# Turned keys of a gated delta-rule chunk loop stored per tile in the key stage and loaded back

## The reference

```
q = silu(hs @ Wq + bq);  k = silu(hs @ Wk + bk);  v = silu(hs @ Wv + bv)
q, k = each scaled to length 1 per head
for every token t, per batch and head (S_f, S_s are 64 x 64):
    S_f = fd_t * S_f;             S_s = sd_t * S_s
    err_f = v_t - k_t @ S_f;      err_s = v_t - k_t @ S_s
    S_f += b_t * outer(k_t, err_f);  S_s += b_t * outer(k_t, err_s)
    S_fc = cap(S_f + rf * S_s);   S_sc = cap(S_s + rf * S_f)
    o_t = fg_t * (q_t @ S_fc) + sg_t * (q_t @ S_sc)
    S_f, S_s = S_fc, S_sc
```

## Time and profile before

| | |
|---|---|
| median of three runs | 3439.89 us (3428.99 to 3453.76) |
| the profiled execution | 3432.23 us, span 3430.6 us |
| PE, PEld, DVE, ACT, POOL busy | 83%, 58%, 74%, 47%, 36% of the span |
| mean granted clock | 0.928 |
| key stage | about 658 to 838 us |
| chunk loop | about 840 to 2400 us |
| DMA | 290.81 MB, mean 85 GB/s |

### The profile page before, as it was taken

One profiled execution on the slowest core, in us unless ns is written; L12 is line 12 of the kernel. 1 busy time (PEld: TensorE's weight loads), 2 busy tenths in 40 slices (PEclk: granted clock), 3 DMA queues, 4 the chain that ended last, 5 costly groups with the idle time before them and its releaser, 6 DMA issues. The chain is left out here.

```text
span 3430.6 us, 74926 instructions
## 1 busy us (share of the span) xinstructions
PE 2858.1 (83%) x28151; PEld 1973.1 (58%) x28151; DVE 2554.0 (74%) x4553; ACT 1598.3 (47%) x3575; POOL 1238.9 (36%) x1882
## 2 busy tenths in 40 slices
PE   0565999685999999999999999999484459998888
PEld 0343544364777777777777777777372443333323
DVE  8897588794787868787787868766597347777775
ACT  1222799784344444444444444434252335555554
POOL 0000233312565656666565656655464230000000
PEclk9876999896999999999999999999697779999999
DMA  1001465686123132323323232222472521011111
GB/s 31 0 0 52 166 246 234 256 259 162 34 74 68 38 83 64 78 44 74 67 71 56 53 83 63 66 45 64 148 259 75 157 60 20 20 29 20 20 26 27
DMA packets 487658, 290.81 MB, mean 85 GB/s; under 512 B 402907, under 2 KB 447515, under 8 KB 478493
## 3 DMA queue, kind: packets, MB, share of 16 engines
q1 hardware_dynamic: 478080, 256.61, 27.5%
q10 hardware_dynamic: 4608, 16.78, 1.6%
q0 software_dynamic: 4608, 12.59, 1.1%
HBM read 155.92 MB, written 129.97 MB: 83 GB/s over the span
## 5 line engine op out<-in xcount | busy, mean ns | idle before, releaser
L2388 DVE TENSOR_REDUCE mx<-banks 128x2 f32<-128x1024 f32 (+3 forms) x384 | 358.2, 955 | 146.0 <-PE banks L1839 95.2
L2080 ACT ACTIVATE probs<-banks 128x1024 f32<-128x1024 f32 (+3 forms) x384 | 309.9, 810 | 257.1 <-PE banks L1864 143.8
L1116 ACT COPY xs<-banks 64x64 f32<-64x64 f32 (+2 forms) x640 | 166.2, 260 | 397.9 <-PE banks L958 394.8
L828 POOL TENSOR_SCALAR xc<-xc,halves 128x64 f32<-128x64 f32 (+1 forms) x256 | 193.9, 757 | 359.4 <-DVE xc L1299 346.5
L958 PE MATMUL banks<-xc,ssm 64*64 64x16 f32 (+2 forms) x5120 | 249.9, 217 | 37.1 <-issue 35.0
L958 PEld LDWEIGHTS banks<-xc,ssm 64*64 64x64 f32 x5120 | 209.7, 135 | 116.4 <-issue 57.7
L1718 PE MATMUL banks<-wproj,xnT 128*128 128x512 f32 x512 | 265.4, 600 | 0.9 <-DVE sb_tok L2165 0.9
L1589 POOL TENSOR_TENSOR prj_sq<-prj 128x1024 f32<-128x1024 f32 x32 | 77.6, 2424 | 490.7 <-ACT prj L1983 490.7
L1299 DVE SCALAR_TENSOR_TENSOR xc<-xc,halves,banks 64x64 f32<-64x64 f32 (+1 forms) x512 | 160.0, 312 | 110.8 <-PE banks L969 104.7
L1106 ACT COPY ssm<-banks 16x64 f32<-16x64 f32 (+2 forms) x896 | 215.9, 241 | 50.4 <-PE banks L930 38.3
L1141 ACT COPY ah<-banks 128x768 f32<-128x768 f32 x128 | 102.2, 798 | 254.4 <-PE banks L990 254.4
(11 more groups left out here) (352 smaller groups left out, 6744.7 us busy)
## 6 DMA issues: line engine op xcount, KB each, us to landing
proj_s<-prj SPq DMA_DIRECT2D x32, 2048.0 KB, 6.7
qkv_t<-proj_s SPq DMA_DIRECT2D x32, 1536.0 KB
ka<-proj_s ACTq DMA_DIRECT2D x32, 512.0 KB, 4.5
mem_s<-o_sb SPq DMA_DIRECT2D x32, 512.0 KB, 2.6
om<-mem_s SPq DMA_DIRECT2D x32, 512.0 KB, 3.8
om<-proj_s SPq DMA_DIRECT2D x32, 512.0 KB, 4.8
nblk_s<-ssa POOLq DMA_DIRECT2D x32, 256.0 KB, 4.2
blk_s<-res SPq DMA_DIRECT2D x16, 512.0 KB, 4.3
```

The lines of the kernel that those rows point to most:

```text
L828: pool.tensor_scalar(inverse_of(k, lv + 1)[:, :, w:2 * w], inverse_of(k, lv), halves[:, lv, 1:2], None, ALU.mult).then_inc(half_set, 1)
L1116: last = act.copy(xs[right, k % 2, 0:4 * (SUB << lv)], products(k, lv, out_)[right, :])
L2080: act.activation(probs[:, s % 2, :, at:at + w], slot_of((kind, s, k))[:, :, 0:w], ACT.Exp, scale=D1 ** -0.5).then_inc(b_read, 1)
L2388: dve.tensor_reduce(mx[:, s % 2, c, :, t:t + 1].rearrange("p e a -> p (e a)"), slot_of((kind, s, k))[:, :, 0:w], AX, ALU.max).then_inc(a_r ...
```

## The change

In the key stage the turned keys, which lie in `kta` anyway, are stored by POOL to a new DRAM tensor `kt_s`, 512 KB per tile. POOL's order becomes: turned keys of tile i, blocks of tile i. ACT waits, before it overwrites a buffer of `kta`, for the store of the tile two before. SP loads the turned keys of tile i (512 KB, in pieces of 512 bytes) into `kqt`, which now holds two whole tiles (16 KB per partition in place of 4 KB; the spare tensor above shrinks so that addresses behind it stay). It does so for tiles 0 and 1 at the end of its table work in the key stage, and for each later tile directly behind the tokens. `turn` makes the two transposes of the queries alone, and `keep_turned` copies 256 columns in place of 512. The scores still read keys and queries side by side.

```diff
+        kt_s = dram("kt_s", (T, P, HD))
-        kqt = sb("kqt", [P, 2, 2, 2, P], scope=sT)
+        kqt = sb("kqt", [P, 2, 4, 2, 2, P], scope=sT)
+        kt_out = stepped
-        TILE_IN = 16 * (6 + 3 * NB)
+        TILE_IN = 16 * (7 + 3 * NB)
+            def load_turned(i):
+                sp.dma_start(kqt[:, i % 2, :, :, 0, :].rearrange("p g a t -> p (g a) t"), kt_s[i].rearrange("p (g t) -> p g t", t=P)).then_inc(tile_in[i % 2], 16)
...
                 sp.dma_start(pcb[64 * e:64 * e + 64, :], pc_s[e, :, :, :].rearrange("t h q -> (t h q)").partition_broadcast(64)).then_inc(pc_in, 16)
+            for i in range(2):
+                sp.wait_ge(kt_out[i], 16)
+                load_turned(i)
             end_phase(sp)
...
             def load_tile(i):
                 load_tokens(i)
+                load_turned(i)
                 load_right(i)
...
                 sp.wait_ge(av_mm, 4 * i - 4)
+                sp.wait_ge(y_mm, 4 * i - 4)
                 sp.wait_ge(s_new, 4 * i - 4)
...
         def chunk_pool(pool):
...
             for i in range(T):
                 n = i % 2
+                pool.wait_ge(kt_kept, 2 * i + 2)
+                pool.dma_start(kt_s[i], kta[:, n, :]).then_inc(kt_out[n], 16)
                 pool.wait_ge(ss_kept, 8 * i + 8)
...
             for n in range(2):
                 pool.wait_ge(nblk_out[n], 16 * (T // 2))
+                pool.wait_ge(kt_out[n], 16 * (T // 2))
             end_phase(pool)
+            for x in kt_out:
+                pool.sem_clear(x)
...
+            def turned(k):
+                return kqt[:, k // 4 % 2, k % 4, :, :, :]
...
             def turn(k):
...
-                for w, at in ((1, 0), (0, 1)):
-                    for p in range(2):
-                        first_col = w * HD + P * (2 * g + p)
-                        last = pe.transpose(cols(bk[1], 2 * p + at), qkv_t[:, n, first_col:first_col + P], ident[:, :])
+                for p in range(2):
+                    last = pe.transpose(cols(bk[1], p), qkv_t[:, n, P * (2 * g + p):P * (2 * g + p) + P], ident[:, :])
...
             def keep_turned_keys(i):
...
                 if i >= 2:
                     act.wait_ge(ss_mm, 2 * i - 2)
+                    act.wait_ge(kt_out[i % 2], 16 * (i // 2))
...
             def keep_turned(k):
...
-                if k >= 2:
-                    act.wait_ge(kq_mm, k - 1)
-                    act.wait_ge(y_mm, k - 1)
-                act.copy(kqt[:, y, :, :, :].rearrange("p a w t -> p (a w t)"), bk[1]).then_inc(kq_kept, 1)
+                if k >= 8:
+                    act.wait_ge(y_mm, k - 7)
+                act.copy(kqt[:, i % 2, k % 4, :, 1, :], bk[1][:, 0:2 * P].rearrange("p (a t) -> p a t", t=P)).then_inc(kq_kept, 1)
```

More of the change, by code:

```diff
@@ L153, in layer_kernel @@
         sA.close()
-        SPARE = 3280
+        SPARE = 208
         sG = ExitStack()
@@ L929, in scores @@
                 for m, h, r, p in heads(k):
-                    last = pe.matmul(bk[m % 2][:, 256 * p:256 * p + 256], kqt[r, k % 2, p, 0, :], kqt[r, k % 2, p, :, :].rearrange("p w t -> p (w t)"),
+                    last = pe.matmul(bk[m % 2][:, 256 * p:256 * p + 256], turned(k)[r, p, 0, :], turned(k)[r, p, :, :].rearrange("p w t -> p (w t)"),
                                      start=True, stop=True)
@@ L979, in states @@
                 for m, h, r, p in heads(k):
-                    last = pe.matmul(cols(bk[2 + m % 2], 2 * w + p), kqt[r, k % 2, p, w, :], S_t[r, 2 * g + p, :], start=(w == 0 and p == 0), stop=(w == 0), skip_group_check=True)
+                    last = pe.matmul(cols(bk[2 + m % 2], 2 * w + p), turned(k)[r, p, w, :], S_t[r, 2 * g + p, :], start=(w == 0 and p == 0), stop=(w == 0), skip_group_check=True)
                 if w:
```

## The result

| | before | changed |
|---|---|---|
| median | 3442.8 us (3428.99 to 3453.76, 4 runs) | 3605.23 us (3599.46 to 3609.41, 4 runs) |
| ratio | | 1.0473, 95% interval 1.0431 to 1.0515 |
| span of the profiled execution | 3430.6 us | 3607.8 us |
| PE's first turn of the loop | 839.90 us | 882.35 us |
| last product of the last `solve` starts | 2411.1 us | 2591.1 us |

The kernel became 4.7% slower. Of the 177.2 us between the two profiles 42.5 lie ahead of the loop's first turn, 137.5 in the loop, and -2.8 behind it. The first is the part that the prediction put at 39.5; the second it put at -3.

The account below looks back on a forecast made before the run. It took ACT's copies and DMA traffic to pace the key stage, and ACT's copy, not PE, to hold the loop's update. Terms -3 + 0 + 4 + 33.5 + 2 = +36.5 on 3432.2 gave 3469, as median 3476 us; range 3446 to 3508.

Parts of the forecast that it names:

- The key stage: Stage before the loop: a 512 KB store per tile and ACT's wait for it cost +33.5 us to tile 26.
- start: Key stage, tiles 0 to 4, while 3 MB of token tiles are loaded: +4 us (0 to 8).
- quiet: Key stage, tiles 4 to 16, ACT setting the pace: 5.03 us per tile, +11.5 us (0 to +19).
- crowded: Key stage, tiles 16 to 26, block stores already landing slowly: 6.9 us per tile for 5.3, +16 us (+8 to +31).
- L: Landing time of the new key store: 5.3 us for tiles 4 to 16, 9 for 16 to 26; up to 3.4 free.
- the prediction's formula: Key stage: time per tile is half of 0.7 us to issue, the store's landing time, and 4.06 us of ACT's work.
- the entry: Loop's start: two loads of turned keys last before the barrier, PE's first turn needing the first: +4 us (2 to 8).
- The two transposes: Loop: two of four transposes per step removed; they fill a wait, so 0 to 6.4 us gained, -3 us taken.
- the small sign: Loop: update(k,2) starts 0.11 us after ACT's copy, 0.06 without transposes in front; if they hold it, 6.4 us gained.
- the store hidden: Rival: the key stage hides most of the new store, +4 to +16 us, 3444 to 3456 us; chance 0.14.
- PE the bound of the loop: Rival: update(k,2) really waits for the transposes in the loop, so 42 us go; chance 0.08.
- The DMA engines full: Rival: DMA engines saturate in the key stage, +70 to +80 us, 3510 to 3520 us; chance 0.12.

Follow-up runs that it names:

- e8: e1 with four buffers of kta in place of two, ACT waiting for the store four tiles before; ratio 1.0080 to the kernel before.
- e1: Kernel before plus only the key stage's stores of turned keys and ACT's wait for them; loop unchanged; ratio 1.0146 to the kernel before.
- e4: Kernel before with two transposes in turn, half-width copy and no added transfer, keys in kqt constant; 3527.7 us, 3404.6 for before beside it.
- e2: Changed kernel without the key stage's stores and waits, loads reading keys that aren't turned; ratio 1.0387 to the kernel before.
- e7: Changed kernel with one more, unread transpose in turn, three in all; 3449.0 us, 3400.2 for the kernel before beside it.
- e16: Changed kernel with one more, unread transpose behind update(k,2), not in turn; 3538.0 us, 3406.7 for the kernel before beside it.
- e5: Kernel before, unchanged, profiled again on the chip of the follow-up runs; 3400.3 us, 3400.2 for the kernel before beside it.

## Why the prediction was wrong

**The key stage: the mechanism right, the sum right by some luck.** Forecast to tile 26: +33.5 us; measured +35.7. The mechanism, a ring of two tiles with the landing in it, is shown by e8, which removes it. By parts the forecast is less good: start +7.4 (forecast 4), quiet +18.1 (11.5), crowded +10.1 (16, and 2 for the clearing). The first two came out 10.0 us above the forecast and the last 7.9 below, and the sum hides it. The store's landing time, L, was put at 5.3 us in the quiet stretch and has a median of 6.1 there (12 stores), which gives 5.4 us per tile by the prediction's formula, where 5.58 were measured. In the crowded stretch L was put at 9, and the median is 5.1 (10 stores). By the formula that would be 4.9 us per tile, less than before's 5.3, yet 6.3 were measured: the formula doesn't hold there, as ACT waited in that stretch before the change too, for the block stores. The figure of 3.2 us for 512 KB by the Trainium skill ("DMA: Bandwidth & Descriptors", Anatomy of one DMA), by which the store would have been hidden, isn't met: 5.4 us stand in this trace, and the measurement decides.

**Behind tile 26 and at the entry:** +3.4 and +3.3 (forecast 2 and 4). The changed kernel against e1, which has the stores but not the two loads, gives 882.35 - 879.0 = 3.3 us for the entry as well.

**Loads in the loop: 0, right.** No turn after the first waits for a transfer, and e4 without them is as slow as e2 with them.

**ACT's copy: 0.** No run takes it by itself. But the full-clock steps of the changed kernel, with the copy of half the width, are 12.12 us in the mean, and those of e7 with the same copy and one transpose more as well, against 12.19 before; more than these 0.06 us it can't be.

**The two transposes: the step that failed.** The prediction read rightly that the turn fills a wait. The 0.06 us just named would be an estimated 8 us over 128 steps, close to the 6.4 of the small sign. But from "they fill a wait" it concluded that taking them away can't cost anything: the bounds of the term were 0 and 6.4 us of gain, and a loss had no price. Yet PE's work in that wait had a use. With half the turn gone PE falls to its lower level in 92 of 128 steps, for 3.4 us in the step shown, just where `solve` and `scores` stand. That is +137.5 us where -3 was forecast. The prediction never asked what a clock of 1.00 rested on. It put that clock among the signs that would confirm the forecast, without a case of its own, and so the range ended 91 us short of the fastest run (3599, against 3508). What a slow `solve` costs could have been priced from the trace of before, whose first step stands at the lower level (clock 0.50) and has 2.93 us where the next has 1.57:

```profile
857.20 2.93 PE L990 MATMUL banks<-stk,tw 128*128 128x192 f32 x8
```

That two missing transposes bring the clock down could not be read from that trace; it only shows, in the key stage, a clock of 0.83 with PE busy 77%. Why the clock falls in this kernel's slow steps and not in the others stays open.

**The rivals:** the store hidden: no. PE the bound of the loop: no, by e7. The DMA engines full: partly at most; the share is 0.94 from 700 to 750 us, and 16 us are left with four buffers (e8).

## What to carry to other kernels

Work that fills a wait on TensorE may not be free to remove where the loop runs at the full clock. Give that a case of its own: price the loop with its longest products at the lower level, and read the granted clock in windows of 1 us over several steps, not as a mean. If such work becomes superfluous, try needed work in its place, near where it stood; here one product of 64 columns served, and two transposes 3 us earlier did not. And where a store joins a ring of buffers, count its landing time against the ring's length first; a deeper ring gave back 23 of 39 us.

## What the runs showed of the hardware that was not expected

- One transpose of 128 x 128 (0.16 us) per step of 12.1 us decides between a mean clock of 1.00 and one of 0.91 (e7 and the changed kernel), and behind the update in place of ahead of it the same transpose gives 0.95 (e16).
- The fall isn't steady: 92 of 128 steps of the changed kernel have it, 7 to 12 in a row, and of two steps with 1.77 and 1.78 us from turn to `solve` one is at the full clock there and one is slow.
- PE's busy share in this profile is 97 to 98% in e1 to e5, with the mean clock at 0.91 and at 1.00; only the granted clock and the durations of single products (326 ns, and a median of 527, for the same form) tell.
- Before's loop has slow steps too, 3 or 4 of 128; with the key stage's part alone (e1) it has 8 and takes 1579.5 us in place of 1571.9, at 0.99.
- Eight small loads of SP take 6.57 us to issue in e5 (DMA share 0.85 meanwhile), 8.58 in the changed kernel (0.86) and 17.29 in e8 (0.93). That the fuller engines slow the issue is a guess from these three.
